# A channel-mixing kernel: the second resident product moved ahead of the third and fourth streamed ones, and the last sums read ahead of the key table

## The reference

```
x = x + x mixed over channels by W0[cond]                 (64x64 per sample)
x = x + mask * (causal long convolution of x with K1 + D1*x)
x = x + (x @ weight^T + bias) + scale * (x @ A^T) @ B^T   (1024x1024 over time, rank 16 adapters, 8 of them)
x = x + mask * (causal long convolution of mask*x with K3 + D3*x)
```

## Time and profile before

| what | value |
|---|---|
| median of 3 runs | 1669.86 us (1668.00 to 1672.62) |
| the profiled execution's own time | 1667.45 us |
| its span, first to last instruction | 1665.7 us |
| granted TensorE clock, mean | 0.974 |
| PE busy | 1517.1 us, 91% |
| DVE busy | 1323.6 us, 79% |
| ACT busy | 742.1 us, 45% |
| POOL busy | 583.7 us, 35% |

### The profile page before, as it was taken

One profiled execution on the slowest core, in us unless ns is written; L12 is line 12 of the kernel. 1 busy time (PEld: TensorE's weight loads), 2 busy tenths in 40 slices (PEclk: granted clock), 3 DMA queues, 4 the chain that ended last, 5 costly groups with the idle time before them and its releaser, 6 DMA issues.

```text
span 1665.7 us, 36843 instructions
## 1 busy us (share of the span) xinstructions
PE 1517.1 (91%) x14983; PEld 1299.6 (78%) x14983; DVE 1323.6 (79%) x1525; ACT 742.1 (45%) x1083; POOL 583.7 (35%) x260
## 2 busy tenths in 40 slices
PE   6777776989999999999999999999999999999998
PEld 6777764778788887887878888787878878878787
DVE  7787877778787878787888888887878787878763
ACT  4435353345353535353545444445353444445443
POOL 2111112615243443425261607080808070616230
PEclk9888897999999999999999999999999999999999
DMA  7799994657575747566666757565757585757532
GB/s 222 274 336 369 330 343 168 147 125 190 118 183 123 185 116 193 122 166 145 147 155 137 166 134 174 124 179 116 179 122 190 105 197 112 199 116 190 119 116 75
DMA packets 455238, 287.62 MB, mean 173 GB/s; under 512 B 331512, under 2 KB 410880, under 8 KB 453056
## 3 DMA queue, kind: packets, MB, share of 16 engines
q1 hardware_dynamic: 405888, 174.57, 46.2%
q10 hardware_dynamic: 49216, 110.98, 19.4%
HBM read 161.30 MB, written 75.96 MB: 142 GB/s over the span
## 4 chain that ended last, share of the span: by engine, by line
DVE 30%; PE 26%; issue 19%; POOL 9%; ACT 7%; DMA 7%; ACTq 1%; DVEq 1%; SPq 0%; POOLq 0%
PE ps L849 7%; PE ps L758 6%; DMA arena<-in_x_dram 5%; DVE arena L1818 4%; DVE arena L1729 4%; DVE arena L1814 3%; PE ps L802 3%; DVE arena L1770 3%; PE ps L706 3%; POOL arena L586 2%; PE ps L768 2%; DVE arena L1777 2%; PE ps L933 2%; POOL arena L582 2%; DVE arena L1760 2%
## 5 line engine op out<-in xcount | busy, mean ns | idle before, releaser
L849 PE MATMUL ps<-arena,w2t 128*128 128x256 f16 x4608 | 528.0, 274 | 37.3 <-DMA w2t<-w_scratch 37.2
L849 PEld LDWEIGHTS ps<-arena,w2t 128*128 128x128 f16 x4608 | 450.3, 98 | 102.0 <-DMA w2t<-w_scratch 45.3
L578 POOL TENSOR_TENSOR arena<-arena 128x1024 f32<-128x1024 f32 x32 | 73.9, 2308 | 858.4 <-DVE arena L1777 767.6
L1818 DVE TENSOR_TENSOR arena<-arena 128x512 f16<-128x512 f32 x128 | 154.4, 1217 | 78.9 <-ACT arena L1273 78.9
L1273 ACT ACTIVATE arena<-arena 128x512 f16<-128x512 f32 x128 | 78.9, 628 | 273.3 <-DVE arena L1814 269.2
L706 PE MATMUL ps<-arena 128*128 128x128 f32 x1024 | 144.1, 303 | 49.2 <-DVE arena L1615 26.2
L706 PEld LDWEIGHTS ps<-arena 128*128 128x128 f32 x1024 | 135.8, 215 | 54.8 <-DVE arena L1615 29.3
L1717 DVE SCALAR_TENSOR_TENSOR arena<-gbuf,arena 128x1024 f16<-128x1024 f32 x64 | 158.8, 2500 | 1.2 <-ACT arena L1194 1.2
L802 PE MATMUL ps<-arena 128*128 128x512 f16 (+1 forms) x768 | 138.3, 331 | 10.2 <-DVE arena L1683 8.2
L1260 ACT ACTIVATE arena<-ps,biasx 128x256 f32<-128x256 f32 x256 | 104.4, 466 | 77.9 <-PE ps L849 73.3
L933 PE MATMUL ps<-arena 128*128 128x256 f16 (+1 forms) x1536 | 137.0, 246 | 0.0
(11 more groups left out here) (239 smaller groups left out, 2698.3 us busy)
## 6 DMA issues: line engine op xcount, KB each, us to landing
w2t<-w_scratch ACTq DMA_DIRECT2D x96, 512.0 KB, 4.5
arena<-in_x_dram SPq DMA_DIRECT2D x64, 512.0 KB, 8.2
out_dram<-arena SPq DMA_DIRECT2D x64, 512.0 KB, 3.4
gbuf<-x_scratch SPq DMA_DIRECT2D x120, 256.0 KB, 4.3
arena<-krow_scratch SPq DMA_DIRECT2D x32, 512.0 KB, 7.4
gbuf<-w_scratch ACTq DMA_DIRECT2D x32, 512.0 KB, 4.8
x_scratch<-arena ACTq DMA_DIRECT2D x14, 1024.0 KB, 9.0
x_scratch<-arena ACTq DMA_DIRECT2D x14, 896.0 KB, 7.3
```

Of the source, the lines that this page charges most:

```text
L849: mm = nc.tensor.matmul(ps[:, bank, n * HW:(n + 1) * HW], weight(p, n, part, k), xx[:, :, k, :], start=(fresh and n == 0 and k == 0 and q ...
L1818: tt(x3_quarter(x3l, h0, row), x3part[slot].rearrange("p (k h b) -> p k h b", k=2, h=2), x3_quarter(x3h, h0, row), ALU.subtract).then_inc( ...
```

## The change

Three orders change, in all bodies.

**PE** (in `stage2`): the two resident(1) products with their deltas, banks `OWN_AT`, and the wait for the split of the low product (`low_hi`, `low_lo`) that goes with them, move ahead of streamed(2) and its wait for the second transformed input. They become sums 5 and 6; the streamed(2) sums become 7 and 8. All later sums keep their number.

**DVE**: the table `OUT_SUMS` gives the sum that each `add_part` waits for: the first two now wait for 5 and 6, not 7 and 8. `add_part(0)`, `add_part(1)` and their splits now stand before `table_lo(0, g+1)`, between the input splits.

**ACT**: `split_hi3(0)` and the third and fourth input split stand before the reads of the streamed(2) sums; then come read 5 with load 5, `split_hi3(1)`, `table_hi(0, g+1)`, read 6 with load 6. At the end `split_hi3(5)` stands before the read of sum 13, and `table_hi(1, g)` moves behind the read of sum 14, `split_hi3(7)` and `state_hi(0, g+1, 0)`. In group 0, `scale_k`, `store_k`, `bases_hi(0, 1)`, `split_k`, `bases_lo(0, 1)` move back too.

```
+        OUT_SUMS = (5, 6, 9, 10, 11, 12)
 # PE
+                pe.wait_ge(low_hi, g + 1)
+                pe.wait_ge(low_lo, g + 1)
+                for p in range(2):
+                    block(OWN_AT[p], p, resident(1), x2_quarter(0, NQ), True, False)
+                    delta(OWN_AT[p], p, 0, left_low, True).then_inc(s2_summed, 1)
                 pe.wait_ge(t_hi, 4 * g + 2)
                 pe.wait_ge(t_lo, 4 * g + 2)
...
-                pe.wait_ge(low_hi, g + 1)
-                pe.wait_ge(low_lo, g + 1)
-                for p in range(2):
-                    block(OWN_AT[p], p, resident(1), x2_quarter(0, NQ), True, False)
-                    delta(OWN_AT[p], p, 0, left_low, True).then_inc(s2_summed, 1)
                 pe.wait_ge(t_hi, 4 * g + 3)
 # ACT
-                for p in range(2):
-                    read_part(g, p, SUM_AT[p], 4, 0, 4, 5 + p)
+                if early:
+                    act.wait_ge(tab_stored[1], 16 * NBLK // 2)
+                split_hi3(g, 0, 0, 0, 0)
+                if more1:
+                    for h in X1_ORDER[2:4]:
+                        x1_split_hi(g + 1, h)
+                read_part(g, 0, SUM_AT[0], 6, 0, 4, 5)
+                split_hi3(g, 1, 0, 2, 1)
+                if more1 and not early:
+                    table_hi(0, g + 1)
+                read_part(g, 1, SUM_AT[1], 6, 0, 4, 6)
                 if early:
                     scale_k(NBLK - 1, 3)
-                    act.wait_ge(tab_stored[1], 16 * NBLK // 2)
                     bases_hi(0, 1)
+                    table_hi(0, 1)
...
+                split_hi3(g, 5, 2, 2, 5)
                 read_part(g, 0, 4, 12, NQ, 0)
-                split_hi3(g, 5, 2, 2, 5)
                 split_hi3(g, 6, 0, NQ, 0)
-                table_hi(1, g)
                 read_part(g, 1, 6, 12, NQ, 0)
                 split_hi3(g, 7, 0, NQ + 2, 1)
...
                     state_hi(0, g + 1, 0)
+                    table_hi(1, g)
                     state_hi(0, g + 1, 1)
 # DVE
-                    dve.wait_ge(s2_summed, NSUM * g + 7 + n)
+                    dve.wait_ge(s2_summed, NSUM * g + OUT_SUMS[n])
...
+                    x1_split_lo(g + 1, X1_ORDER[0])
+                add_part(0, 0, 0)
+                if more1:
+                    x1_split_lo(g + 1, X1_ORDER[1])
+                lo3(0, 0, 0, 0)
+                add_part(1, 1, 1)
+                if more1:
+                    for h in X1_ORDER[2:4]:
                         x1_split_lo(g + 1, h)
+                lo3(1, 0, 2, 1)
+                if early:
+                    split_k(NBLK - 1)
                     bases_lo(0, 1)
                 if more1:
                     table_lo(0, g + 1)
```

More of the change, by code:

```diff
@@ L1337, in body @@
                 split_hi3(g, 2, 2, NQ, 2)
+                if early:
+                    store_k(NBLK - 1)
                 act.wait_ge(s2_summed, NSUM * g + 10)
@@ L1349, in body @@
                     load_w(1)
+                split_hi3(g, 5, 2, 2, 5)
                 read_part(g, 0, 4, 12, NQ, 0)
-                split_hi3(g, 5, 2, 2, 5)
                 split_hi3(g, 6, 0, NQ, 0)
-                table_hi(1, g)
                 read_part(g, 1, 6, 12, NQ, 0)
                 split_hi3(g, 7, 0, NQ + 2, 1)
+                if not more1:
+                    table_hi(1, g)
                 if more1:
                     state_hi(0, g + 1, 0)
+                    table_hi(1, g)
                     state_hi(0, g + 1, 1)
@@ L1821, in body @@
                 if more1:
-                    for h in X1_ORDER[0:2]:
+                    x1_split_lo(g + 1, X1_ORDER[0])
[6 more added lines that the diff above has]
+                    for h in X1_ORDER[2:4]:
                         x1_split_lo(g + 1, h)
+                lo3(1, 0, 2, 1)
                 if early:
+                    split_k(NBLK - 1)
                     bases_lo(0, 1)
@@ L1827, in body @@
                     table_lo(0, g + 1)
-                add_part(0, 0, 0)
-                if early:
-                    split_k(NBLK - 1)
-                if more1:
-                    x1_split_lo(g + 1, X1_ORDER[2])
-                lo3(0, 0, 0, 0)
-                add_part(1, 1, 1)
-                if more1:
-                    x1_split_lo(g + 1, X1_ORDER[3])
-                lo3(1, 0, 2, 1)
                 add_part(2, 4, 2)
@@ L1849, in body @@
                 lo3(6, 0, NQ, 0)
+                lo3(7, 0, NQ + 2, 1)
                 if not more1:
                     table_lo(1, g)
-                lo3(7, 0, NQ + 2, 1)
                 if more1:
```

## The result

| what | before | after |
|---|---|---|
| median of 4 runs each | 1668.93 us | 1648.78 us (1647.23 to 1650.18) |
| profiled execution, own time | 1667.45 us | 1649.81 us |
| its span | 1665.7 us | 1647.9 us |
| granted TensorE clock, mean | 0.974 | 0.978 |
| period of groups 1 to 13, mean | 86.24 us | 85.07 us |

The ratio is 0.9878, with a 95% interval of 0.9855 to 0.9902: faster by 1.2%, some 20 us. The prediction was 1643 us (1634 to 1662). The spans differ by 17.8 us. By the starts of POOL's first instructions, group 0 gives 3.8 (87.21 to 83.40), groups 1 to 13 give 15.3 (1121.16 to 1105.88) and the end 1.2; stage 0 took 2.5 longer. The change does not touch stage 0, and in the 13 kept traces, all with the same stage 0, POOL's first instruction of group 0 starts anywhere from 303.5 to 309.2 us: this part is scatter.

What follows compares the result with a forecast made beforehand. The bound was taken as the cycle DVE, POOL, DVE, ACT's read 8, PE's states. 14 x 1.45 = 20.3 us plus 7 for group 0 made 27.3 off 1667.45: 1640.2; plus 2.4 for the median, 1643 us (1634 to 1662).

Steps and rivals of the forecast that it cites:

- The bound: Middle group: the cycle DVE, POOL, DVE, ACT's read 8, PE's states sets the period of 86.24 us, not PE alone.
- PE's part: PE's sums: load waits of 1.15 and 0.85 us go, 1.3 and 0.5 us come before sums 9 and 10.
- loses 1.9 and gains 2.0: PE's balance of waits in a group, said to bring it to the second state block 0.5 us earlier, at 1126.2.
- DVE's part: DVE up to add_part(5): 0.9 us earlier a group, 0.55 idle time and 0.35 better turns with POOL; bounds 0.4 and 1.5.
- each form kept its duration: Alternative for DVE: durations belong to the instruction's form, only 0.55 us goes; steady groups give 1.2 us instead of 1.5.
- ACT's end, 0.55 us: ACT before read 8: the table's 1.4 us taken out, 0.85 given back by the read behind the split; 0.55 a group.
- Group 0, 7 us: First group: PE's 8.32 us wait at the first table goes; ends 0 and 10.3, taken as 7 us.
- The sum: Whole kernel: 20.3 us from fourteen groups and 7 from the first, 27.3 us off the execution's own time of 1667.45.
- A: PE's new stalls bind: reads 5 and 6 come 1 us later, 0.8 us gained a group, about 1654; chance 0.18.
- B: The group's second half gives the gain back: 0.3 us a group, about 1663, or nothing, 1668; chance 0.14.
- C: Slower: loads 5 and 6, issued behind ACT's splits and table, land late; 1677 us at 7.5 us landing; chance 0.08.

Runs made afterwards that it cites:

- e4: The changed kernel with DVE's add_part(3), (4) and (5) each one place earlier, ahead of lo3(2), lo3(3) and lo3(4): 1618.8 us, ratio 0.970.
- e10: The changed kernel with the last three full-size instructions of POOL's second table made for one of four channels, part of the computation left out: 1619.1 us, ratio 0.969.
- e6: The changed kernel with ACT's read 5 ahead of the third and fourth input split and read 6 ahead of split 1 and the table: 1647.0 us, ratio 0.987.
- e5: The changed kernel with PE's old order (streamed(2) as sums 5 and 6) and its counters; ACT and DVE keep the new order: 1650.0 us, ratio 0.989.
- e2: The kernel before with only ACT's end changed: split 5 ahead of sum 13's read, second table behind split 7 and the first state: 1660.7 us, ratio 0.996.
- e3: The changed kernel with ACT's end of stage 2 put back as it was before: 1656.7 us, ratio 0.993.
- e1: The kernel before with PE's new order and its two counters alone; ACT and DVE keep their old orders: 1723.8 us, ratio 1.034.
- e8: The kernel before with DVE's add_part(3) to (5) one place earlier and nothing else: 1643.2 us, ratio 0.985.
- e7: The changed kernel with both add_part(3) to (5) one place earlier on DVE and ACT's reads 5 and 6 earlier: 1600.3 us, ratio 0.959.

## Why the prediction was right, and where it was off

**The bound.** Right: the cycle DVE, POOL, ACT's read 8, PE's states. e4 and e10 each shorten one member of it and take 30 us off, down to the same period (83.2), at which PE in the steady groups no longer waits for read 8; e6 shortens PE's waits at its sums and takes nothing.

**PE's part.** Right in kind: no wait for loads 3 and 7, new waits before sums 9 and 10. Their size was too high (1.3 and 0.5; measured 0.68 and 0.38). I had laid out load 5 as ACT time between the input splits and read 5; it goes out 2 us before they end and costs ACT nothing. This left PE 1.04 us of slack where I had 0.4. That the PE order matters so little (e5, 0.27 us a group) follows from it, but the prediction did not say so. Its "loses 1.9 and gains 2.0" does not give the 0.5 us by which it lets PE arrive earlier; the sums laid out one by one do, because a wait in a row is shorter than what it costs (the block at 1093.52 was due at 1092.21 and is listed with 1.15).

**DVE's part, 0.9 us a group: mis-sized, 0.63.** The 0.9 was 0.55 of idle time and 0.35 from turns that fall better. The idle time went in full; the turns gave 0.08. From the low difference to `add_part(3)` the four input splits, the three `lo3`, the table and the turned rows take 21.16 us together before and 21.16 after, though single ones changed much (the table 2.85 to 1.75, the turned rows 1.54 to 2.83). From the low difference to the end of the table my layout holds to 0.05 us: `add_part(2)` was laid out at 29.6 us from POOL's start and stands at 29.64. The error is at the place where POOL waits for the table. I let it start with the table's end and take 1.8 us; it starts 0.16 us later and takes 1.93, and the two DVE instructions behind it carry this on. With the 0.04 that the next point lacks, this is the shortfall of 0.3 a group, 3.6 us in 13.

The prediction also named what would come if each form kept its duration, 1.2 us a group; by its own terms (0.55 and 0.55) that is 1.1. The measured 1.15 lies there, not at 1.45, so the period alone would not tell the two apart. The durations do: they moved with their place beside POOL, and in e10 they shrank with POOL's work.

**ACT's end, 0.55 us: right,** 0.51, and e2 and e3 give it alone and together. Behind the first state the table costs nothing.

**Group 0, 7 us: mis-sized, 3.8.** The state block came 6.3 us earlier from POOL's start (46.72 to 40.41), close to the 7. But PE had then stood for 4.01 us, and the stretch behind it to the next group is 2.5 us longer (40.49 to 42.99), the 2.6 of the three slow rows. In the kernel before, the low clock came in the sums, ahead of that block, where it cost 1.95 us (4.74 less 2.79). I had moved the stall away and not asked where the next one would stand.

**The sum.** 27.3 us were forecast on the span and 17.8 came: 3.6 short in groups 1 to 13, 3.2 in group 0, 0.25 in the end, and 2.5 by which stage 0 was longer. The runs' medians differ by 20.2 us.

**Rivals.** A is refuted by e6. B: the second half, from the second state block to the next start of POOL, took 41.17 us (1169.23 - 1128.06 = 41.17) before and 41.16 after; nothing was given back. C: no wait for a load is left in the steady groups. That a late load can make this order slower is shown by e1, where ACT's order is not changed with PE's; there it is load 7, late by its issue and not by its landing.

## What to carry to other kernels

Find the cycle before the busiest engine: PE was busy 91% of the time, and its new order was worth 0.27 us in a group of 85 while DVE and ACT set the pace. An instruction that needs nothing but a finished sum goes ahead of one that waits for another engine's answer; e8 gave 26 us with that alone. And an edit that is worth nothing behind a cover is to be tried again once the cover is gone, as e6 in e7. Where an order may leave the matrix engine standing for some microseconds, count the slow block behind the wait too: in e1 it was half of the loss.

## What the runs showed of the hardware

- Transfers on ACT's queue go out ahead of ACT instructions that stand before them in the program: load 5 at 1088.32, with 2.2 us of earlier ACT work still to run.
- DVE and POOL take turns with one instruction each: a DVE split begun beside a POOL instruction ends 0.55 us behind it with 512 columns (1104.50 and 1103.95) and 1.07 us with 1024 (1100.19 and 1099.12, before). A DVE copy with a single SBUF input takes part: 2.83 us behind POOL's full-size addition in the change, 1.54 behind its last instruction in the kernel before and in e10, and 0.68 in e1 with POOL idle. The adds, which read PSUM, take 0.68 us throughout.
- After 4.01 us of idle time in group 0 PE ran at a granted clock of 0.50 in the window 349 to 352; in the steady groups waits of 1 us do nothing of the sort. In e1 waits of 6.0 to 6.3 us were followed by a slow block in all 14 groups. In e8 both waits of 2.2 us were (4.46 us instead of 2.78) and one of 1.66 was not, yet neither was the one of 3.19 us in group 0 of e5. The length of the wait alone does not decide it.
